# Gathers of a graph-attention kernel on GpSimd: the optional ones moved into the middle of a block, and a block's first one made to wait for the landing of the block before

## What is computed

```python
xp = (layernorm(x) @ W).reshape(n, 4, 64)                      # projection, 4 heads
a_src, a_dst = einsum(xp, att_src), einsum(xp, att_dst)
alpha = leaky_relu(a_src[src] + a_dst[dst])                    # an edge's score
w = softmax of alpha over the edges of each target
x = x + elu(segment_sum(xp[src] * w, dst) + bias)              # <- the gather xp[src]
weights = layernorm(x) @ wr;  idx = top_k(weights, n // 2)     # the routed half
y = (gelu(sel @ w1 + b1) @ w2 + b2) * weights                  # FFN, 256 -> 1024 -> 256
x = x + layernorm(x) + y at idx
```

## Time and profile before

| | |
|---|---|
| three timed runs | 2206.24, 2207.0, 2209.57 us |
| the profiled execution: its span, first to last instruction | 2573.5 us; no other time of it is given, and it is 366.5 us over the median of the timed runs |
| PE / DVE / POOL / ACT busy in it | 77% / 61% / 60% / 29% |
| gathers | 1563, mean 968 ns |
| granted TensorE clock, mean | 0.87 |

### The profile page before, as it was taken

One profiled execution on the slowest core, in us unless ns is written; L12 is line 12 of the kernel. 1 busy time (PEld: TensorE's weight loads), 2 busy tenths in 40 slices (PEclk: granted clock), 3 DMA queues, 4 the chain that ended last, 5 costly groups with the idle time before them and its releaser, 6 DMA issues.

```text
span 2573.5 us, 29095 instructions
## 1 busy us (share of the span) xinstructions
PE 1981.2 (77%) x9511; PEld 1633.8 (63%) x9512; DVE 1581.4 (61%) x3510; ACT 744.5 (29%) x1478; POOL 1554.5 (60%) x1626
## 2 busy tenths in 40 slices
PE   8935877877877877878778877877777777877787
PEld 6723666666666666666666666666666666666666
DVE  4555655665655655656656665666665665666576
ACT  4512222222322222322232232232232232223223
POOL 2366666666666666666666666666666666666630
PEclk9967988888888889889888888988988988889889
DMA  8844444444444444444444444444444444444447
GB/s 287 276 143 121 123 134 124 132 138 120 137 138 118 132 135 124 135 140 120 134 137 128 130 136 124 134 134 130 128 134 131 127 139 124 131 136 136 119 159 312
DMA packets 157137, 369.12 MB, mean 143 GB/s; under 512 B 46646, under 2 KB 73682, under 8 KB 155699
## 3 DMA queue, kind: packets, MB, share of 16 engines
q0 software_dynamic: 75088, 208.19, 30.1%
q1 hardware_dynamic: 74706, 145.62, 16.9%
q10 hardware_dynamic: 7184, 13.41, 1.4%
HBM read 328.20 MB, written 38.89 MB: 143 GB/s over the span
## 4 chain that ended last, share of the span: by engine, by line
POOL 38%; issue 23%; PE 19%; another core or an unknown queue 9%; DVE 3%; DMA 3%; ACT 2%; POOLq 1%; DVEq 0%; SPq 0%; ACTq 0%
POOL rows L692 38%; PE ag_ps L1057 7%; PE h_ps L1021 4%; PE ag_ps L934 3%; PE y_ps L1040 3%; DMA rows<-node_rows,ends 3%; POOLq L402 1%; DVE oh L1366 1%; DVE rows L1404 1%; ACT hT L808 1%; PE ag_ps L1128 0%; ACT L808 0%; PE ag_ps L1129 0%; ACT L812 0%
## 5 line engine op out<-in xcount | busy, mean ns | idle before, releaser
L692 POOL DMA_INDIRECT rows<-node_rows,ends x1563 | 1512.9, 968 | 850.6 <-issue 482.5
L1057 PE MATMUL ag_ps<-rows,oh 128*128 128x260 f32 x3518 | 845.9, 401 | 47.5 <-DVE rows L1404 34.8
L1021 PE MATMUL h_ps<-xnT,w1s 128*128 128x256 f32 x1568 | 534.0, 500 | 419.2 <-DVE zz L1385 227.1
L1057 PEld LDWEIGHTS ag_ps<-rows,oh 128*128 128x128 f32 x3518 | 716.7, 204 | 180.3 <-DVE rows L1404 37.8
L1021 PEld LDWEIGHTS h_ps<-xnT,w1s 128*128 128x128 f32 x1568 | 377.0, 250 | 517.9 <-DVE zz L1385 234.8
L1404 DVE TENSOR_TENSOR rows<-rows,xl_ps 128x512 f32<-128x512 f32 (+3 forms) x392 | 503.1, 1346 | 47.2 <-issue 26.5
L1385 DVE TENSOR_TENSOR zz<-rows,edge_dm 128x72 f32<-128x72 f32 x98 | 22.9, 233 | 695.0 <-DMA rows<-node_rows,ends 656.4
L1040 PE MATMUL y_ps<-w2s,hT 128*128 128x256 f32 x1568 | 368.0, 386 | 12.2 <-DVE oh L1366 9.2
L831 ACT COPY rows<-rows 128x780 f32<-128x780 f32 x97 | 81.6, 842 | 998.6 <-DMA rows<-node_rows,ends 998.6
L1040 PEld LDWEIGHTS y_ps<-w2s,hT 128*128 128x128 f32 x1568 | 301.7, 194 | 66.7 <-DVE oh L1366 16.6
L1366 DVE TENSOR_TENSOR oh<-xl_ps,dloc 128x2304 f32<-128x2304 f32 x98 | 249.0, 2541 | 0.0
(11 more groups left out here) (243 smaller groups left out, 1433.7 us busy)
## 6 DMA issues: line engine op xcount, KB each, us to landing
dbc<-dst SPq DMA_DIRECT2D x97, 576.0 KB
rows<-node_rows,ends POOLq DMA_INDIRECT x1563
selfr<-node_rows SPq DMA_DIRECT2D x98, 130.0 KB
base<-in_x SPq DMA_DIRECT2D x14, 896.0 KB, 7.1
base<-in_x SPq DMA_DIRECT2D x49, 256.0 KB
ffn_rows<-yb ACTq DMA_DIRECT2D x48, 256.0 KB
node_rows<-base SPq DMA_DIRECT2D x13, 910.0 KB, 5.7
base<-in_x_turned SPq DMA_DIRECT2D x14, 384.0 KB, 7.7
```

Source lines behind the costliest of these rows:

```text
L692: pool.indirect_dma_start(out=rows[:, b, t, :], out_offset=None, in_=table, in_offset=bass.IndirectOffsetOnAxis(ap=ends[:, b, t, 0:1], axi ...
L1021: last = nc.tensor.matmul(h_ps[:, m * PAIR:(m + 1) * PAIR], w1s[:, c, n * P:(n + 1) * P], xnT[:, c, :], start=(c == 0), stop=(c == DC - 1))
L1057: product = nc.tensor.matmul(ag_ps[b][:, 0:ROW], oh[:, b, t, :], rows[:, b, t, :], start=(t == 0), stop=False)
```

## The change

The optional gathers of a block (from block 2 on) are issued after tile 8 and not at the block's end; they wait for `carry_ok` alone. `y_ok` is waited for nowhere on POOL. Before tile 3, from block 3 on, POOL waits until all 15 obligatory gathers of the block before have landed. In the written-out path each wait is set on the gather itself (`held`); where two waits stand before one gather, one stays an instruction of its own. Besides, three loads of table entries now state their bounds in `value_load`: `optional_landed` is the one that runs here, on VectorE, once a block.

```diff
-    LOOKED_UP, SUMMED, SECOND_LAYER = 4, (8, 11, 13), TILES - 2
+    LOOKED_UP, SUMMED, OPTIONAL = 4, (8, 11, 13), 5
         def optional_landed(eng, w):
-            landed = eng.value_load(win[0:1, bass.ds(COLS * w + 7, 1)])
-            return nc.s_assert_within(landed, 16, 16 * (NW + 3), skip_runtime_bounds_check_because="...")
+            return eng.value_load(win[0:1, bass.ds(COLS * w + 7, 1)], min_val=16, max_val=16 * (NW + 3))
+            def held(w, semaphore, value):
+                if isinstance(w, int):
+                    pool.wait_ge(semaphore, value)
+                else:
+                    wait_apart(pool, (semaphore, value))
             def follow(w, started):
                 if started == LOOKED_UP:
-                    wait_apart(pool, (lk_ok, w + 1))
+                    held(w, lk_ok, w + 1)
                 for k in range(GROUPS):
                     if started == SUMMED[k]:
-                        wait_apart(pool, (freed[k], w))
-                if started == SECOND_LAYER and known(w, 5) and not (isinstance(w, int) and w == NW - 1):
-                    wait_apart(pool, (y_ok, w - 4))
+                        held(w, freed[k], w)
             def window(w, i, b):
+                def optional(known_w):
+                    if known_w >= 1:
+                        held(w, carry_ok, w)
+                    some = entry(pool, w, 5, 2)
...
+                        with pool.If(some > 0):
+                            gather(2, gath_last[b])
+                        with pool.If(some > 1):
+                            gather(1, gath_last[b])
                 for t in range(3, tiles_of(w)):
-                    if known(w, 2) and t == 3:
-                        wait_apart(pool, (ld_ends[b], 16 * (i + 1)))
+                    if t == 3:
+                        if known(w, 3):
+                            held(w, gath[1 - b], 16 * (TILES - 3) * (i + b))
+                        held(w, ld_ends[b], 16 * (i + 1))
                     if known(w, 1):
                         follow(w, t - 3)
                     gather(t, gath[b])
-                if known(w, 1):
-                    wait_apart(pool, (carry_ok, w))
-                    follow(w, TILES - 2)
-                some = entry(pool, w, 5, 2)
...
+                    if known(w, 2) and t - 3 == OPTIONAL:
+                        optional(2)
+                if not known(w, 2):
+                    optional(w)
```

More of the change, by code:

```diff
@@ L403, in entry, with counted_before @@
                                       skip_runtime_bounds_check_because="the window table holds counts and places of the edges' tiles, which lie within their number")
+        def counted_before(eng, w, k):
+            return eng.value_load(win[0:1, bass.ds(COLS * w + k, 1)], min_val=0, max_val=NW * EP // P)
         def optional_landed(eng, w):
-            landed = eng.value_load(win[0:1, bass.ds(COLS * w + 7, 1)])
-            return nc.s_assert_within(landed, 16, 16 * (NW + 3), skip_runtime_bounds_check_because="a parity's first node block has one gather or more, each later one two at most")
+            return eng.value_load(win[0:1, bass.ds(COLS * w + 7, 1)], min_val=16, max_val=16 * (NW + 3))
         def all_extra(eng):
@@ L420, in for_extra @@
                 with eng.If(n > 0):
-                    before = entry(eng, w, 2, NW * EP // P)
+                    before = counted_before(eng, w, 2)
                     with eng.Fori(0, n) as j:
@@ L433, in if_exact @@
                     n = entry(eng, w, 3, EP // P)
-                    before = entry(eng, w, 4, NW * EP // P)
+                    before = counted_before(eng, w, 4)
                     with eng.If(n > 0):
@@ L674, in exact_gather @@
                 gather_row(k, m_row, m_go)
+            def held(w, semaphore, value):
[3 more added lines that the diff above has]
+                    wait_apart(pool, (semaphore, value))
             def follow(w, started):
                 if started == LOOKED_UP:
-                    wait_apart(pool, (lk_ok, w + 1))
+                    held(w, lk_ok, w + 1)
                 for k in range(GROUPS):
                     if started == SUMMED[k]:
-                        wait_apart(pool, (freed[k], w))
-                if started == SECOND_LAYER and known(w, 5) and not (isinstance(w, int) and w == NW - 1):
-                    wait_apart(pool, (y_ok, w - 4))
+                        held(w, freed[k], w)
             def window(w, i, b):
-                if not known(w, 2):
-                    pool.wait_ge(ld_ends[b], 16 * (i + 1))
                 def gather(t, arrived):
@@ L693, in gather @@
                                             in_offset=bass.IndirectOffsetOnAxis(ap=ends[:, b, t, 0:1], axis=0)).then_inc(arrived, 16)
+                def optional(known_w):
+                    if known_w >= 1:
+                        held(w, carry_ok, w)
+                    if known_w < 1:
+                        pool.wait_ge(win_ld, 16)
+                    some = entry(pool, w, 5, 2)
+                    if known_w < 1:
+                        gather(2, gath_last[b])
+                        with pool.If(some > 0):
+                            gather(1, gath_last[b])
+                        with pool.If(some > 1):
+                            gather(0, gath_last[b])
+                    elif known_w < 2:
+                        gather(2, gath_last[b])
+                        with pool.If(some > 1):
+                            gather(1, gath_last[b])
+                    else:
+                        with pool.If(some > 0):
+                            gather(2, gath_last[b])
+                        with pool.If(some > 1):
+                            gather(1, gath_last[b])
                 for t in range(3, tiles_of(w)):
-                    if known(w, 2) and t == 3:
-                        wait_apart(pool, (ld_ends[b], 16 * (i + 1)))
+                    if t == 3:
+                        if known(w, 3):
+                            held(w, gath[1 - b], 16 * (TILES - 3) * (i + b))
+                        held(w, ld_ends[b], 16 * (i + 1))
                     if known(w, 1):
@@ L700, in window @@
                     gather(t, gath[b])
-                if known(w, 1):
-                    wait_apart(pool, (carry_ok, w))
-                    follow(w, TILES - 2)
-                if not known(w, 1):
-                    pool.wait_ge(win_ld, 16)
-                some = entry(pool, w, 5, 2)
[L709 to L725, removed]
+                    if known(w, 2) and t - 3 == OPTIONAL:
+                        optional(2)
+                if not known(w, 2):
+                    optional(w)
                 if isinstance(w, int) and w == 0:
```

## The result

Before 2208.28 us (2206.24 to 2211.26), after **2377.51 us** (2376.24 to 2381.23), four runs of each: ratio 1.0768, 95% interval [1.0752, 1.0783]. The forecast was 2355, with a range from 2250 to 2403. The profiled execution of after has a span of 2374.5 us, as long as its timed runs; that of before was 366 longer than its own.

A forecast was written before the change was run, and what follows sets the result against it. POOL, issuing gathers without spare time, was taken as the bound: 132.5 + 1563 x 1.254 + 91.1 = 2184 us, plus 171 for the landing's wait in 95 blocks, gives 2355 us, range 2250 to 2403.

The forecast's parts named there:

- The landing's wait: Before tile 3, POOL waits for tile 17's landing: gap 2.1 us instead of 0.30, 95 blocks, +171 us (+149 to +219).
- The long gaps: POOL's gaps of some 3 us at about every twelfth gather, 368 us, taken as only the profiled execution's.
- The rival of gathers cheaper when not profiled: Gathers on POOL take 0.968 us when not profiled, so dropping `y_ok` frees PE's loop: 2057 us; chance 0.16.
- The base of the sum: POOL's time without the new wait: 132.5 + 1563 x 1.254 + 91.1 = 2184 us.
- the loop through PE: Optional gather to `zz`, PE's work, next optional gather: 20.26 us a block against POOL's 20.06; 98 blocks give 2209.
- `y_ok`, up to 20 us: Dropping POOL's wait for `y_ok` is worth 0.2 us a block, 20 us, at most 23.
- The optional gathers, moved: Optional gathers behind tile 8: same number, same 1.254 us each, `carry_ok` and table load covered; worth 0.
- Which lands as the optional one did: Tile 17, now the last gather before `zz`, was said to land as the optional gather had.
- Waits on the gathers and bounds: Five separate waits a block on POOL moved onto gathers, and bounds in VectorE's load (0 to 0.3 us a block): 0.
- The tests: Signs expected in the profile after: 2.0 to 2.6 us gaps before tile 3, 1.25 elsewhere, no `y_ps` wait, more PE idling.
- half of the pauses absorbed: Half of the 95 pauses at tile 3 fall together with real long gaps: +85 us, 2270; absorption in part has chance 0.08.
- its three chances: POOL pays the landing in each block 0.76; part of it absorbed 0.08, of which 0.02 within 0.2%; cheaper gathers 0.16.

The follow-up runs named there:

- kernel 1: The changed kernel without the landing's wait before tile 3, everything else of the change kept: 1.0072 of before, 2229.7 us.
- kernels 5 to 7: The kernel before with bounded loads only (1.0026 of before), then also with waits on the gathers (1.0009), then also without `y_ok` (1.0001).
- kernel 7: The kernel before with bounded loads, waits on the gathers and no `y_ok`; optional gathers last, no landing's wait: 1.0001 of before, 2210.7 us.
- experiments 7 and 8: `y_ok` dropped with optional gathers last, bounds and waits on gathers (1.0001); `y_ok` put back into the changed kernel without landing's wait (1.0077).
- kernel 12: The changed kernel without the landing's wait, one-hots in the form that writes a sum, residual's intermediate in PSUM: 0.9986 of before, 2208.2 us.
- kernels 11 and 12: Both kernel 1 with sum-writing one-hots; 11 also has the minimum as SCALAR_TENSOR_TENSOR (1.0066 of before), 12 the residual's intermediate in PSUM (0.9986).

## Why the prediction was right, step by step, and where it was not

**The landing's wait: right.** Forecast a gap of 2.1 us (2.0 to 2.6), 95 times, +171 us; measured 2.10 on average, 95 times, +169.1 over the gaps of kernel 1. Its two parts, 1.87 + 0.25, measured 1.80 + 0.26 in the rows shown: the value chosen near the lower end of the unknown start held. The Trainium skill's figure for the fixed part of such a DMA ("DMA: Bandwidth & Descriptors", section on the anatomy of one DMA by the GpSimd path) would have made the time some 48 us less; the trace has 2.75 us from the start to the news, and the measurement decides.

**The long gaps belong to one profiled execution: right**, and the riskiest choice: the profiles of all thirteen later kernels have spans within 7 us of their timed medians, those with the same waits too. The cause is not known. That it is PE's news that is late rests on one gap, at `lk_ok`; the earlier trace rows put 24 gaps, 79.6 us, down to ScalarE's copy.

**The rival of gathers cheaper when not profiled does not hold.** Kernel 1 did not go to 2057.

**The base of the sum: the step that failed.** I took 1.254 us for every gather, from a stretch without a stall, and got 2184, "only 23 under the median". The mean of all gathers stood in the earlier trace rows: 968 ns; with 0.30 that is 1563 x 1.268 = 1982, and + 224 = 2206, the timed runs with nothing left over. (The gap is nearer to 0.305, which makes it 2213; with the 964 ns of kernels 5 to 7, whose gathers stand in the same order, it is 2207.) The 23 us were gathers held up by VectorE, not the loop through PE: in kernel 7, which has no `y_ok`, the gathers take 1506.8 us where 1563 x 0.949, what is left of 1.254 without the gap, is 1483.3. In the kernel after it is much the same: its gathers take 1503.1 us, 19.8 more than that. These 20 us are what my sum was too low by against the span of 2374.5; its idle time came out within 2 us of the forecast.

**`y_ok`, up to 20 us: wrong, 0** (the table of experiments 7 and 8). The agreement of 98 x 20.26 + 224 with the median within 0.1% was a coincidence of two sums: 16 x 1.268 is 20.29 a block, and without the wait the loop cannot bind, yet the time stays.

**The optional gathers, moved: costed at nothing, wrong by itself.** They cost 0.7% without the landing's wait, through gathers held up. "Which lands as the optional one did" missed VectorE's load between the two waits, which now comes after the landing. In the kernel after this did not show: with a pause of 2.1 us a block POOL and VectorE stand to each other otherwise, the gathers beside the residual are 121 at 0.990 us where kernel 1 has 183 at 1.032, and the mean gather is 962. That the term came out at nothing there was luck.

**Waits on the gathers and bounds: 0, right** within what was measured (1.0009 [0.9995, 1.0023] together).

**The tests.** No wait put down to PE's `y_ps` or any PE work: so. 1.25 between other gathers: so, in median. The optional gather sixth behind tile 3: so by the code; no row names it. PE idle before `hidden` some 2 us longer a block: partly. Its idle time is 350.9 us after and 244.9 in kernel 7, 1.1 more a block; the rest of the pause went into longer matmuls: PE is busy for 1936.8 us at a mean granted clock of 0.898 (a mean over its two levels, 1.2 and 2.4 GHz), in kernel 7 for 1872.8 us at 0.944. No gather waited for that.

**Two slips in the forecast's own numbers.** Its sum for half of the pauses absorbed is 2270, its range calls 2250 the half-absorbed case; and its three chances add up to 0.82 slower and 0.16 faster where it says 0.81 and 0.17. Neither touches the outcome.

## What to carry to other kernels

When one engine issues without a pause, put its instructions' busy time, the usual gap and everything else into one account from the means of the whole trace, not from a clean stretch: the difference between mean and clean stretch is a cost with a cause of its own. A wait on the landing of the instruction just issued costs the landing less what can be issued in between; here two gathers made the same wait free. And moving an instruction moves what it hid: the optional gather at the block's end covered both the landing and a table load on another engine.

## What the runs showed of the hardware

VectorE instructions of 256 columns that read two SBUF tensors, and the fast TENSOR_SCALAR over int16 (2304 columns in 0.84 us), can hold up a gather that GpSimd issues at the same time: 1.01 to 1.09 us on average in the table above, 1.04 to 1.17 in the rows shown, where 0.95 is usual. Whether they do depends on where in the gather they fall: 68 gathers of kernel 7 beside such an addition took 0.946. The 0.23 us instructions of 72 columns behind `zz`, also with both inputs in SBUF, left it at 0.946 beside 76 to 88 gathers each in kernel 7 (`zl`, `zc`). The same TENSOR_SCALAR in the form that writes a sum (2.60 us) and instructions with one of their inputs in PSUM don't: 0.946 in all three rows of kernel 12. It goes both ways: `dbc` takes 0.81 us, but 0.96 where it starts 0.6 to 0.7 us behind a gather (26 times in kernel 1, those gathers 1.003).

The Trainium skill ("SBUF — State Buffer", section "Who interferes with whom") gives the rule: VectorE and GpSimd share a pair of ports. A VectorE instruction in a two-port mode takes the pair whole; one with two SBUF inputs contends with a GpSimd instruction that reads SBUF, because its second input comes through the shared read side. The runs agree on both kinds (`dbc` 1.06 to 1.08 beside its fast form and 0.946 to 0.959 beside the one with a sum; the residual 1.093 and 0.946, kernels 11 and 12, at the same place in the gather), though no row names the mode that an instruction ran in. The page also infers that a `tensor_tensor` does not stall the writing of descriptors; for these indirect gathers, whose indices lie in SBUF, that does not hold: the gather at 1048.27 of kernel 1 meets no other instruction with both inputs in SBUF than two TENSOR_TENSORs, and takes 1.17 us. The runs decide.
